# Hybrid conv/attention/MoE kernel: the last two expert units summed by TensorE, the last stores on two DMA-issuing engines, gates turned by the transpose instruction

## The reference

```python
logits = einsum('bsd,de->bse', x, gate_w) + gate_b      # x = layernorm(t), 16 experts
top_probs, top_idx = top_k(softmax(logits), 2)
dispatch = sum(one_hot(top_idx, 16) * (top_probs / sum(top_probs))[..., None], axis=-2)
hidden = silu(einsum('bsd,edh->bseh', x, w1)) * einsum('bsd,edh->bseh', x, w2)
out = einsum('bseo,bse->bso', einsum('bseh,eho->bseo', hidden, w3), dispatch)
t = t + out
return tokens back to (batch, channel, y, x)
```

## Time and profile before

| what | us |
|---|---|
| median of 3 runs (lowest to highest) | 491.02 (489.63 to 494.27) |
| profiled execution, its own device time | 486.73 |
| its span, first to last instruction | 484.9 |
| mean granted TensorE clock (share of full speed) | 0.982 |

### The profile page before, as it was taken

How to read it: one execution, slowest core, us unless ns; L and a number is a source line. 1 busy time by engine, 2 the same in 40 slices (tenths; PEclk the granted TensorE clock), 3 DMA queues, 4 the chain that set the end, 5 groups by cost and what they waited for, 6 DMA issues and landing times.

```text
span 484.9 us, 9115 instructions
## 1 busy us (share of the span) xinstructions
PE 434.6 (90%) x2998; PEld 303.3 (63%) x2998; DVE 347.4 (72%) x1090; ACT 283.1 (58%) x676; POOL 175.6 (36%) x305
## 2 busy tenths in 40 slices
PE   2999999999968988979999988999989888998994
PEld 1787777767467887979898944344435444545542
DVE  4178998867777656788978853637666888797862
ACT  3467776732557876758788855765655333343431
POOL 4400001203134563383793342415341454343342
PEclk9998999999989998989999999999999999999998
DMA  7300000000400000012300004212112213041330
GB/s 178 144 2 1 2 0 1 1 2 0 87 3 1 1 2 1 2 39 51 69 20 3 1 3 141 63 39 68 43 38 74 68 45 105 28 122 66 99 102 11
DMA packets 13567, 20.94 MB, mean 43 GB/s; under 512 B 4592, under 2 KB 6384, under 8 KB 13008
## 3 DMA queue, kind: packets, MB, share of 16 engines
q1 hardware_dynamic: 13056, 19.99, 14.4%
q10 hardware_dynamic: 464, 0.37, 0.3%
HBM read 19.62 MB, written 0.72 MB: 42 GB/s over the span
## 4 chain that ended last, share of the span: by engine, by line
PE 63%; DVE 16%; ACT 8%; issue 6%; POOL 4%; DMA 2%; POOLq 0%; DVEq 0%; SPq 0%; ACTq 0%
PE PS L2171 14%; PE PS L1871 7%; PE PS L1909 6%; PE PS L2182 5%; PE PS L2193 5%; PE PS L1930 3%; PE PS L2103 3%; PE PS L2091 2%; PE PS L1829 2%; PE PS L1998 2%; PE PS L2013 2%; PE PS L2047 2%; ACT score_arena L968 2%; DVE QL L1468 2%; DVE score_arena L1577 2%
## 5 line engine op out<-in xcount | busy, mean ns | idle before, releaser
L2171 PE MATMUL PS<-YTs,WH 64*128 64x512 f32 x192 | 77.0, 427 | 1.9 <-ACT VV L1067 1.6
L735 POOL TENSOR_TENSOR pr<-pr 128x512 f32<-128x512 f32 x39 | 50.4, 1291 | 75.9 <-DVE pr L1630 44.7
L2171 PE MATMUL PS<-YX,WH 64*128 64x512 f32 x192 | 77.2, 426 | 0.0
L968 ACT ACTIVATE score_arena<-score_arena,nmx 128x128 f32<-128x128 f32 (+1 forms) x128 | 56.9, 446 | 22.2 <-DVE nmx L1577 21.8
L1067 ACT ACTIVATE VV<-PS 128x512 f32<-128x512 f32 x64 | 35.4, 595 | 41.6 <-PE PS L2171 41.5
L1023 ACT ACTIVATE stage<-PS,wk 128x512 f32<-128x512 f32 x64 | 40.8, 684 | 22.8 <-PE PS L2171 22.7
L1743 DVE TENSOR_TENSOR stage<-VV,PS 128x512 f32<-128x512 f32 x64 | 41.8, 682 | 17.1 <-ACT VV L1067 12.5
L2171 PEld LDWEIGHTS PS<-YTs,WH 64*128 64x128 f32 x192 | 35.3, 184 | 29.6 <-ACT VV L1067 12.6
L908 ACT ACTIVATE st_mem<-PS 128x512 f32<-128x512 f32 x72 | 37.3, 612 | 18.5 <-PE PS L1909 18.5
L2103 PE MATMUL PS<-cst,score_arena 128*128 128x128 f32 x192 | 34.4, 290 | 6.6 <-ACT score_arena L968 6.1
L2091 PE MATMUL PS<-YTs,QH 128*128 128x128 f32 (+1 forms) x128 | 38.9, 328 | 0.0
(11 more groups left out here) (277 smaller groups left out, 1130.1 us busy)
## 6 DMA issues: line engine op xcount, KB each, us to landing
QH<-gate_store SPq DMA_DIRECT2D x96, 128.0 KB, 2.9
stage<-in_wexp SPq DMA_DIRECT2D x6, 512.0 KB, 5.9
wk<-in_w SPq DMA_DIRECT2D x1, 1034.0 KB, 9.8
wa<-in_wat SPq DMA_DIRECT2D x1, 768.0 KB, 8.1
out<-X SPq DMA_DIRECT2D x16, 32.0 KB, 1.9
cst<-in_consts SPq DMA_DIRECT2D x1, 483.0 KB, 6.4
wc<-in_w SPq DMA_DIRECT2D x2, 183.5 KB, 5.8
score_arena<-in_wcv SPq DMA_DIRECT2D x2, 144.0 KB, 6.2
```

The source lines that it names most:

```text
L735: nc.gpsimd.tensor_tensor(acc[:, c % 2], acc[:, c % 2], weighted[:, u % 2], ALU.add).then_inc(acc_added, 1)
L968: ins = nc.scalar.activation(PR[:, s % 3, cols], MS[:, s % 3, cols], ACT.Exp, bias=nmx[:, s % 3, qt:qt + 1], scale=-1.0, accum_out=rsum[:, ...
L2171: ins = mm(PS[:, banks[i], :], w[hs, m, tiles[i] * P:(tiles[i] + 1) * P], ys[i][hs, cs], start=(k == 0), stop=(k == 2))
```

## The change

1. GpSimd no longer adds unit u = 46. `token_sum("fE", 3)` now waits for the adds up to u = 45, does its four products on `acc`, and stands ahead of `second_out(31)`. A new function `last_units`, behind `second_out(31)`, adds four products on the buffer of u = 46 and four on that of u = 47 to the same bank.
2. Of the last chunk's four stores, SyncE issues two and ScalarE the other two; ScalarE also waits for all stores at its end.
3. `gate_turn` uses the transpose instruction in place of the matmul with the identity.

```diff
-            def store(c):
+            def store(c, halves=(0, 1)):
 
                 sp.wait_ge(misc_free, FILL["oT", c] + 1)
-                for h in range(2):
+                for h in halves:
                     for pt in range(PT):
                         sp.dma_start(out[h * J + c, :, pt * P:(pt + 1) * P], X[pt * C:(pt + 1) * C, c, h * P:(h + 1) * P]).then_inc(stored, 16)
...
-            store(J - 1)
+            store(J - 1, (0,))
             sp.wait_ge(stored, 16 * J * 2 * PT)
...
             for r in range(UNITS3):
-                if r >= 1:
+                if 1 <= r < UNITS3 - 1:
                     add_unit(UNITS2 + r - 1)
...
             output(3)
+            act.wait_ge(misc_free, FILL["oT", J - 1] + 1)
+            for pt in range(PT):
+                act.dma_start(out[2 * J - 1, :, pt * P:(pt + 1) * P], X[pt * C:(pt + 1) * C, J - 1, P:2 * P]).then_inc(stored, 16)
+            act.wait_ge(stored, 16 * J * 2 * PT)
...
             def token_sum(name, c):
                 late = name == "fE" and c == 3
-                if late:
-                    pe.wait_ge(acc_added, added(UNITS2 + UNITS3 - 1))
-                else:
-                    pe.wait_ge(acc_added, added(PAIRS2 * (c + 1) if name == "fC" else UNITS2 + PAIRS3 * (c + 1)))
+                units = UNITS2 + UNITS3 - 2 if late else PAIRS2 * (c + 1) if name == "fC" else UNITS2 + PAIRS3 * (c + 1)
+                pe.wait_ge(acc_added, added(units))
                 take(name, c)
                 for q in range(CHUNK):
-                    ins = mm(PS[:, 7, q * C:(q + 1) * C], acc[:, c % 2, q * P:(q + 1) * P], c_("halves"), start=True, stop=not late)
-                    if late:
-                        if q == 0:
-                            pe.wait_ge(combined, UNITS2 + UNITS3)
-                        ins = mm(PS[:, 7, q * C:(q + 1) * C], weighted[:, (UNITS2 + UNITS3 - 1) % 2, q * P:(q + 1) * P], c_("halves"), start=False, stop=True)
+                    ins = mm(PS[:, 7, q * C:(q + 1) * C], acc[:, c % 2, q * P:(q + 1) * P], c_("halves"), start=not late or q == 0, stop=not late)
+                if not late:
+                    ins.then_inc(misc_filled, 1)
+
+            def last_units():
+
+                for u in (UNITS2 + UNITS3 - 2, UNITS2 + UNITS3 - 1):
+                    pe.wait_ge(combined, u + 1)
+                    for q in range(CHUNK):
+                        ins = mm(PS[:, 7, q * C:(q + 1) * C], weighted[:, u % 2, q * P:(q + 1) * P], c_("halves"), start=False,
+                                 stop=u == UNITS2 + UNITS3 - 1 and q == CHUNK - 1)
                 ins.then_inc(misc_filled, 1)
...
                 for q in range(CHUNK):
-                    ins = mm(PS[0:E, 7, q * P:(q + 1) * P], gate[:, m, 4 * c + q, 0:E], ident, start=True, stop=True)
+                    ins = nc.tensor.transpose(PS[0:E, 7, q * P:(q + 1) * P], gate[:, m, 4 * c + q, 0:E], ident)
                 ins.then_inc(misc_filled, 1)
...
+            token_sum("fE", 3)
             second_out(UNITS3 - 1)
-            token_sum("fE", 3)
+            last_units()
             result(3)
```

## The result

The changed kernel's median is 485.39 us (482.3 to 486.95, 8 runs) against 490.79 us (487.83 to 494.27, 8 runs). The ratio is 0.9912, with a 95% interval of 0.9884 to 0.994: 0.9% faster (the quotient of the two medians alone is 0.989). The prediction was 487.3 us against 491.02, a ratio of 0.9925.

What follows compares the result with a forecast made beforehand. PE was taken to bound the kernel, busy 90% of the span with 63% of the chain. Gate turns 2.2, last sum 0.5 and stores 1.0 sum to 3.7 us off 491.02: 487.3 us, range 484.3 to 490.5 us.

Steps and rivals of the forecast that it cites:

- What bounds the kernel: Whole kernel: PE, busy 90% of the span and holding 63% of the chain, so what TensorE executes counts.
- Size of a gate turn: Each gate turn: four transposes take 0.53 us against 0.97 us for eight records, saving 0.44 us (bounds 0.38 and 0.52).
- Rival (b): Gate turns: a narrow transpose is far cheaper than a wide one, 0.24 us per four; 485.1 us, chance 0.15.
- The other two count nothing, because the DMA wait covers them.: Second and third gate turns: 0.9 us of PE time saved counts nothing, hidden by DMA of the first gates.
- I take 15% off.: Six gate turns on the chain: 2.6 us cut to 2.2 us for savings ending in waits for another engine.
- Rival (a): Gate turns: their savings end in waits for DVE and DMA; 489.0 us, chance 0.24 together with Rival (d).
- The last sum: Tail: products on `acc` fill half their length in PE's idle gap, saving 0.5 us (bounds 0 and 0.9).
- Rival (d): Tail: late GpSimd add of unit 45 or slower store landing takes the gain back; 488.8 us, 0.24 with Rival (a).
- The stores: End of kernel: four stores on two queues take 2.7 instead of 3.7 us, saving 1.0 us (bounds 0.3 and 1.2).
- Rival (c): Behind gate turns: the clock falls, 1.7 us lost each; four falls give 494.1 us, chance 0.05.
- The signs of being wrong: Last `combine` starting on a GpSimd wait, new clock falls between 280 and 470, or first gate turn-to-470 shortening under 1 us.
- The sum: Whole kernel: gate turns 2.2, last sum 0.5 and stores 1.0 make 3.7 us, giving 487.3 us.

Runs made afterwards that it cites:

- the changed kernel's second profile: The changed kernel run again with nothing altered, on the same chip as its parts: median 484.12 us, ratio 0.9857 to the kernel before.

## Why the prediction was right, and where it wasn't

- **What bounds the kernel.** PE time on the chain counts. Shown by the transposes done twice, which gave back what the transposes had gained. It counts one for one only where the chain stays on PE, as below.
- **Size of a gate turn.** 0.53 us and a saving of 0.44 us were forecast, between bounds of 0.45 and 0.60; the rows say 0.53 to 0.54. Rival (b), far cheaper narrow transposes, is refuted: half the records at the old pace is what they cost.
- **"The other two count nothing, because the DMA wait covers them."** Wrong. The cover was one slow landing in the one profile that I read, 3.48 us against 1.5 in the others. All three gate turns of that stretch count: 11.90 to 10.58 us, 1.32 us instead of 0.44. The first one's saving does not run through the two DMAs either, but through PE and ScalarE's copy into the second gate turn.
- **"I take 15% off."** About right for what is lost in waits (0.4 us), but a gain was missed. The stretches T4 to T5 and T8 to take show the full 0.43 us, T7 to T8 0.36 us. T5 to T6 gave 1.23 us, because VectorE's subtraction now comes ahead of GpSimd's add and no longer behind it. Only T6 to T7 gives far less. With one fall in each, it took 29.82 and 29.78 us with products, and 29.73 and 29.74 us with transposes: under 0.1 us. The first twelve records of hidden products behind T6 show where most of it goes, in the chain of the kernel before and of the changed kernel's second profile:

```profile
389.56 1.58 PE PS L2171 x12
```

```profile
386.37 0.89 PE PS L2179 x6
387.26 0.02 issue
387.29 0.96 PE PS L2179 x6
```

They take 1.87 us instead of 1.58, so 0.3 of the 0.44 us end in a wait at once. The gate turns together were forecast at 2.2 us and gave 3.3 ± 0.5. Rival (a) holds for this one gate turn and is refuted for the whole.
- **The last sum.** Forecast 0.5 us, measured 0.37 to 0.40 us in the profiles, by the mechanism forecast: a filled gap of half a microsecond. The margin of 0.2 us by which GpSimd's add of unit 45 is ready held. Rival (d) is refuted by the stretches; the runs of the two parts of the tail alone (0.0 ± 0.5 and 0.6 ± 0.6 us) would not do it.
- **The stores.** Forecast 1.0 us with 2.1 us to the last landing; measured 1.0 us in the profile, with 1.8 and 2.1 us to landing.
- **Rival (c), the clock.** The falls exist and cost what was estimated (1.6 us against 1.7), and the changed kernel's profile holds two of them in this stage. But over all runs the mean clock of the changed kernel is higher (0.9774 and 0.9813 against 0.9753), not lower. The falls of this stage stand where PE has just waited or soon after, with products as well as with transposes, and vary between runs of one kernel. The rule of the Trainium skill on transposes and the clock ("TensorE: Matmul & The Clock Gate", "Part 4: PE-mode transpose") shows no cost in any run here. Why the changed kernel falls less often was not tried; its shorter wait near 360, where kernels with the long one often fall, is a candidate.
- **The signs of being wrong.** Two of the three that the prediction named came up in the first profile: two falls between 280 and 470, and no shortening from the first gate turn on (T1 to T8 is 166.35 us against 166.30). They were badly chosen. The kernel with only the new sum, which has no gate turn as transposes, has three falls in that stretch, and two falls cost more than the change gains there.
- **The sum.** 3.7 us forecast, 4.3 ± 0.6 at equal clock. The parts: 1.1 us too little for the gate turns, about 0.1 to 0.5 too much for the tail. The raw medians differ by 5.4 us, beyond the 2.5 to 4.9 us of the forecast, since the clock was higher as well. The two things that the prediction missed, two gate turns (0.9 us) and the dodged collision in T5 to T6 (0.8 us), make more than the 0.6 us between 3.7 and 4.3. Added up over stretches without falls, the change is worth 5.2 us, while the runs say 4.3 in both sets; why they give 0.9 us less is open. So that the forecast came so near is in part luck.

## What to carry to other kernels

Replace an fp32 product with the identity by the transpose instruction where TensorE is on the chain of waits: it saves one of two records, worth 0.11 us each for these narrow tiles, and TensorE time is all that it saves. A wait for a DMA in a single profile is weak evidence of cover, as one landing can be 2 us off; look for the same transfer elsewhere in the trace before counting work behind it as free. When runs of one kernel scatter by more than the effect, compare at equal granted clock and by stretches between landmarks, not by spans.

## What the runs showed of the hardware that was not expected

- A VectorE tensor operation of 0.42 us with both operands in SBUF is held when a GpSimd tensor operation is already under way: three of the nine of line 1438 took 1.50, 1.28 and 0.91 us in the kernel before, and about 0.42 us once GpSimd waits. In the other order GpSimd's takes longer, 1.45 instead of 1.27 us. On the chain this cost 2.4 ± 0.5 us, more than two of the three parts of the change. VectorE's operations that read PSUM beside GpSimd's adds don't show it: line 1630 takes 0.677 to 0.692 us in all 32 cases, 11 of them beside an operation of GpSimd.
- The time of a run moves with its mean granted clock, by 0.37 us per 0.001 over the runs of this case, and a fall between T6 and T7 costs 1.6 us.
- Two stores issued at the same moment on SyncE's and ScalarE's queues land in 1.8 and 2.1 us, against 1.9 us from one queue alone.
